# A four-layer megakernel: the first pair's split and first convolution made one stage earlier, and the second pair's moved among the edge products

## What is computed

```python
x = x + ffn0(cond0(x, cond_512))   # fp8-quantised 1024x1024 product
x = x + ffn1(cond1(x, cond_512))   # 1024x1024 product and a top-2 mixture of 16 low-rank experts
x = x + ffn2(cond2(x, cond_512))   # the same with sparsemax over 8 experts
x = x + ffn3(cond3(x, cond_512))   # low rank, gated (SiLU), low rank

def cond(x, style):                # TYPES = same, upsample, same, downsample
    for i, typ in enumerate(TYPES):
        x = layer(x, style, weights[i], biases[i], mod_w[i], mod_b[i], typ)
```

## Time and profile before

| | |
|---|---|
| median of 3 runs | 2204.11 us (2204.09 to 2206.6) |
| the profiled execution | 2207.09 us |
| its span in the trace | 2205.3 us |
| TensorE busy | 2032.4 us, 92% |
| VectorE, ScalarE, GpSimd busy | 54%, 40%, 18% |
| mean granted TensorE clock | 0.964 of full speed |

### The profile page before, as it was taken

One profiled execution on the slowest core, in us unless ns is written; L12 is line 12 of the kernel. 1 busy time (PEld: TensorE's weight loads), 2 busy tenths in 40 slices (PEclk: granted clock), 3 DMA queues, 4 the chain that ended last, 5 costly groups with the idle time before them and its releaser, 6 DMA issues. The chain is left out here.

```text
span 2205.3 us, 29894 instructions
## 1 busy us (share of the span) xinstructions
PE 2032.4 (92%) x9742; PEld 1665.3 (76%) x9750; DVE 1183.8 (54%) x1986; ACT 885.6 (40%) x1366; POOL 388.3 (18%) x463
## 2 busy tenths in 40 slices
PE   4899956899999979997999999988999999979998
PEld 4777723788888868886788888867888778858886
DVE  6888888745445443224644445436555444454443
ACT  4577722444433321002433333324666544413441
POOL 4122211111111100012111111111000033342334
PEclk9999989899999989997999999998999999989999
DMA  7666546321112232224311111212111011132114
GB/s 185 187 182 181 167 162 216 101 75 57 57 57 71 63 124 76 77 95 135 99 57 57 57 57 61 63 49 81 29 38 33 15 53 50 46 132 78 50 43 156
DMA packets 96302, 196.97 MB, mean 89 GB/s; under 512 B 16768, under 2 KB 46976, under 8 KB 95488
## 3 DMA queue, kind: packets, MB, share of 16 engines
q1 hardware_dynamic: 94976, 194.40, 28.2%
q10 hardware_dynamic: 1280, 1.97, 0.4%
HBM read 142.27 MB, written 54.07 MB: 89 GB/s over the span
## 5 line engine op out<-in xcount | busy, mean ns | idle before, releaser
L936 PE MATMUL ps<-l_u_hi,l_g_hi 128*128 128x512 f32 x512 | 208.9, 408 | 15.7 <-DVE l_u_lo L1270 10.1
L1100 ACT ACTIVATE l_hs<-ps,l_EY,dem3e 128x512 f32<-128x512 f32 x128 | 99.2, 778 | 302.4 <-PE ps L936 292.4
L936 PE MATMUL ps<-l_u_lo,l_g_hi 128*128 128x512 f32 x512 | 204.7, 400 | 0.0
L936 PE MATMUL ps<-l_u_hi,l_g_lo 128*128 128x512 f32 x512 | 204.2, 399 | 0.0
L119 POOL TENSOR_TENSOR l_hs<-l_EY,ones 128x4 f32<-128x4 f32 x128 | 35.0, 273 | 860.1 <-ACT l_hs L1100 860.1
L989 PE MATMUL ps<-l_w_hi,l_h_hi 128*128 128x512 f32 x512 | 167.7, 409 | 0.0
L989 PE MATMUL ps<-l_w_lo,l_h_hi 128*128 128x512 f32 x512 | 163.7, 401 | 0.0
L989 PE MATMUL ps<-l_w_hi,l_h_lo 128*128 128x512 f32 x512 | 163.1, 400 | 0.0
L2228 POOL TENSOR_TENSOR f_a_lo<-f_prod,f_a_hi 128x512 fp32r<-128x512 f32 (+1 forms) x88 | 113.8, 1293 | 269.2 <-ACT f_a_hi L2131 269.2
L2184 DVE SCALAR_TENSOR_TENSOR f_prod<-ps,b,f_gate 128x512 f32<-128x512 f32 (+1 forms) x88 | 66.0, 750 | 170.0 <-ACT f_gate L2124 170.0
L1270 DVE SCALAR_TENSOR_TENSOR l_u_lo<-ps,s_u,l_u_hi 128x512 fp32r<-128x512 f32 x128 | 95.5, 749 | 89.1 <-ACT l_u_hi L1082 88.9
(11 more groups left out here) (326 smaller groups left out, 4892.3 us busy)
## 6 DMA issues: line engine op xcount, KB each, us to landing
xin<-x SPq DMA_DIRECT2D x96, 256.0 KB, 4.0
l_xr<-x SPq DMA_DIRECT2D x32, 512.0 KB, 4.6
x<-l_xr SPq DMA_DIRECT2D x32, 512.0 KB, 2.6
v<-in_ffn_v SPq DMA_DIRECT2D x84, 128.0 KB, 2.7
xin<-in_x SPq DMA_DIRECT2D x16, 512.0 KB, 5.5
xb<-in_x SPq DMA_DIRECT2D x16, 512.0 KB, 3.2
x<-xb SPq DMA_DIRECT2D x16, 512.0 KB, 2.6
q_xr<-x SPq DMA_DIRECT2D x16, 512.0 KB, 3.9
```

What stands on the lines that cost most here:

```text
L936: mm = nc.tensor.matmul(ps[:, 3 + h, :], Gs[ws][:, h, at:at + P], Us[ms][:, h, 1 + q:1 + q + HALF], start=(k == 0), stop=(k == 11))
L1100: nc.scalar.activation(hs[:, h, :], ps[:, 3 + h, :], ACT.Identity, bias=EY[:, 1, 0, bass.ds(h * NP + p, 1)], scale=dem3e[:, bass.ds(h * NP ...
```

## The change

It has five parts.

1. `Xs`, `Zs` and a tile `rows` become constants of the whole program. At the end of `fp8_ffn`, `expert_delta` and of layer 2's conv phase, ScalarE (`split_first_hi`) and VectorE (`split_first_lo`) make the splits of x and z for pair 0 of the layer that follows, and TensorE (`first_conv0`) its first convolution. In layers 1 to 3 the phase itself then begins without them.
2. The waits for the last stores at the end of `fp8_ffn`, `expert_delta` and the conv phases go. In their place there are waits in the next stage: SP's ahead of the load of the bias, ahead of the pack (`c_raw`), GpSimd's ahead of a memset, ScalarE's ahead of hs, VectorE's ahead of `expert_delta`'s first output.
3. In every layer's first pair `weights_a(1)` and the first half of pair 1's convolution (`conv0_half(1, 0)`) come before `edges_p`, the second half behind `edges_v`, and `weights_a(2)` before `edges_y`. VectorE makes x_lo of pair 1's first half ahead of its part of `edges_u`; ScalarE waits for `m_done` before `read_u(1, h)`.
4. TensorE waits for the memsets (`zeros_ready`) before `weights_g(0)` in layers 1 to 3, and GpSimd no longer clears the borders of `Xs` there.
5. Several tiles share memory: `hs`, `xr`, `bias_n`, `ve_f` and the outputs of the feed-forward stages are parts of `rows`.

```diff
+    def split_first_lo(self, nc, dve, n, sem):
+
+        for h in range(2):
+            dve.wait_ge(sem("xh_ready"), 2 * NP * n + h + 1)
+            nc.vector.scalar_tensor_tensor(self.Xs[1][:, h, 1:HALF + 1], self.xin[:, h, :], self.s_x[:, n, h:h + 1],
+                                           self.Xs[0][:, h, 1:HALF + 1].bitcast(F32), ALU.mult,
+                                           ALU.subtract).then_inc(sem("xl_ready"), 1)
...
+    def first_conv0(self, nc, pe, ps, n, sem):
+
+        pe.wait_ge(sem("clo_ready"), n)
+        pe.wait_ge(sem("ul_ready"), 2 * NP * n)
+        for h in range(2):
+            pe.wait_ge(sem("xl_ready"), 2 * NP * n + h + 1)
+            k = 0
+            for t in range(2):
+                for ws, ms in PASSES:
+                    mm = nc.tensor.matmul(ps[:, h, :], self.c_part[ws][:, B0 + t * P:B0 + (t + 1) * P],
+                                          self.Xs[ms][:, h, t:t + HALF], start=(k == 0), stop=(k == 5))
+                    k += 1
+            mm.then_inc(sem("c0_done"), 1)
...
             if with_ffn:
+                sp.wait_ge(sem(("q_stored0", "e_stored0")[layer - 1]), 8 * NP)
                 sp.dma_start(bias_n[:, :], d[f"ffn{layer}_bias"].partition_broadcast(P)).then_inc(bias_loaded, 16)
...
             if with_ffn:
                 store(NP - 1)
-                sp.wait_ge(x_stored, 16 * (r0 + NP))
...
-            pe.wait_ge(zeros_ready, 2 * layer + 1)
-            if layer > 0:
-                pe.wait_ge(clo_ready, layer)
-            conv0(0)
+            if layer == 0:
+                pe.wait_ge(zeros_ready, 1)
+                conv0(0)
             weights_a(0)
             edges_u()
+            pe.wait_ge(zeros_ready, 2 * layer + 1)
             weights_g(0)
...
                 if first:
+                    weights_a(1)
+                    conv0_half(1, 0)
                     edges_p()
-                    weights_a(1)
                     main(0)
                     edges_v()
-                    conv0(1)
+                    conv0_half(1, 1)
+                    weights_a(2)
                     edges_y()
                     weights_g(1)
                     transpose_h(0)
-                    weights_a(2)
...
+                act.wait_ge(m_done, 2 * g0 + 1)
                 read_u(1, 0)
+                act.wait_ge(m_done, 2 * g0 + 2)
                 read_u(1, 1)
...
-            split_x(0)
+            if layer == 0:
+                split_x(0)
             edges_x()
-            split_z(0)
+            if layer == 0:
+                split_z(0)
             read_u(0, 0)
             read_u(0, 1)
             read_a(0)
             split_z(1)
+            split_x_half(1, 0)
             dve.wait_ge(zeros_ready, 2 * layer + 2)
             edges_u()
             some_maxima(1)
             sum_g(0)
-            split_x(1)
+            split_x_half(1, 1)
             split_g(0)
...
             quantise(NP - 1, 1, False)
             finish(NP - 2, 0, False)
+            K.split_first_lo(nc, dve, 1, sem)
             finish(NP - 1, 1, False)
```

More of the change, by code:

```diff
@@ L147, in __init__, with split_first_hi @@
         self.c_raw = tile("c_raw", [P, CW])
+        self.Xs = [tile("x_hi", [P, 2, HALF + 2], F32R), tile("x_lo", [P, 2, HALF + 2], F32R)]
+        self.Zs = [tile("z_hi", [P, 2, TAPS, C], F32R), tile("z_lo", [P, 2, TAPS, C], F32R)]
+        self.rows = tile("rows", [P, 2, L])
+    def split_first_hi(self, nc, act, n, sem):
+        act.wait_ge(sem("x_loaded"), 32 * NP * (n - 1) + 32)
+        act.wait_ge(sem("c0_done"), 2 * NP * n)
+        for h in range(2):
+            nc.scalar.activation(self.Xs[0][:, h, 1:HALF + 1], self.xin[:, h, :], ACT.Copy,
+                                 scale=self.s_x[:, n, h:h + 1]).then_inc(sem("xh_ready"), 1)
+        act.wait_ge(sem("a_done"), NP * n)
+        for h in range(2):
+            nc.scalar.activation(self.Zs[0][:, h, :, :], self.Z[:, n, :, :], ACT.Copy,
+                                 scale=self.s_v[:, n, h:h + 1]).then_inc(sem("zh_ready"), 1)
@@ L564, in conv_phase @@
         else:
-            stage = kept["b_raw"] if layer == 1 else sb("stage", [P, SLOTS, KB * SMALL[2] if layer == 2 else L])
+            stage = kept["b_raw"] if layer == 1 else sb("stage", [P, SLOTS if layer == 2 else 2, KB * SMALL[2] if layer == 2 else L])
         if with_ffn:
@@ L621, in conv_phase @@
         if with_ffn:
-            xr = sb("xr", [P, L])
+            xr = K.rows[:, 0, :]
         chunks = []
@@ L760, in _ @@
                     load_chunk(k)
+                if layer == 3:
+                    sp.wait_ge(sem("x_stored"), 16 * r0)
+                else:
+                    for s in range(2):
+                        sp.wait_ge(sem(("q_stored", "e_stored")[layer - 1] + str(s)), 8 * NP)
             if with_ffn:
@@ L1052, in _ @@
             over_pairs(pe, iteration)
+            if layer == 2:
+                K.first_conv0(nc, pe, ps, 3, sem)
             if layer == 3:
@@ L1176, in first_pair @@
                     act.wait_ge(sem("p_packed_away"), 48)
+                elif layer < 3:
+                    act.wait_ge(sem(("q_stored1", "e_stored1")[layer - 1]), 8 * NP)
                 read_h(0, 0)
@@ L1221, in iteration @@
                     next_weights()
+                    if layer == 2:
+                        K.split_first_hi(nc, act, 3, sem)
                 if layer > 0:
@@ L1457, in tail @@
                     v.tensor_copy(tau[:, 0:1], tau[:, 0:1]).then_inc(small_read, 1)
+                if layer == 2 and isinstance(p, int) and p == NP - 1:
+                    K.split_first_lo(nc, dve, 3, sem)
                 if with_ffn:
@@ L1573, in _ @@
             g = nc.gpsimd
-            for t in Xs:
-                step(g.memset(t[:, :, 0:HALF + 2:HALF + 1].bitcast(F32), 0.0))
+            if layer == 0:
+                for t in Xs:
+                    step(g.memset(t[:, :, 0:HALF + 2:HALF + 1].bitcast(F32), 0.0))
             step(g.memset(g_f[0:C, :, 0:C], 0.0))
@@ L1683, in _ @@
             store(NP - 1, 1)
-            for s in range(2):
-                sp.wait_ge(stored[s], 8 * NP)
         @block.gpsimd
@@ L1703, in _ @@
             turns(act, body)
+            K.split_first_hi(nc, act, 1, sem)
         @block.vector
@@ L1787, in expert_delta @@
         xr = sb("xr", [P, 2, L])
-        xo = sb("xo", [P, 2, L])
+        xo = K.rows
         b_dram = d["ffn1_b"].rearrange("(k p) o -> k p o", p=P)
@@ L1911, in finish @@
                 dve.wait_ge(xr_loaded[s], 8 * (p - s) + 16)
+                if first and s == 0:
+                    dve.wait_ge(sem("x_stored"), 16 * NP)
                 if not first:
@@ L1984, in gated_ffn @@
         prod = sb("prod", [P, 2, HALF])
-        asp = [sb("a_hi", [P, 2, HALF], F32R), sb("a_lo", [P, 2, HALF], F32R)]
+        asp = [t[:, :, 0:HALF] for t in K.Xs]
         zsp = [sb("z_hi", [P, 2, T], F32R), sb("z_lo", [P, 2, T], F32R)]
         xr = sb("xr", [P, NT, L])
-        xo = sb("xo", [P, 2, L])
+        xo = K.rows
         (const_loaded, w_hi, w_lo, v2_hi, v2_lo, gu_done, silu_ready, prod_ready, ah_ready, al_ready,
```

55 lines of the change are left out of this document (35 added, 20 removed).

## The result

The changed kernel takes 2198.13 us (median of 10 runs, 2195.07 to 2200.84), the kernel before 2204.27 in the runs made beside it (10 runs, 2199.76 to 2208.04). The ratio is 0.9971, 95% interval 0.9962 to 0.9980: 6 us faster. The number forecast was 2192.7 with a range of 2185 to 2200. So the sign and the range held, and the size was half of what the sum gave. The profiled execution took 2199.35 us (span 2197.5), 7.7 less than that of before.

A forecast was written before the change was run, and what follows sets the result against it. TensorE, busy 92% of the span, was taken as the bound, leaving its idle and low-clock stretches. Terms summed to -11.4 us, taking the profiled 2207.09 to 2195.7 us and the median to 2192.7; range 2185 to 2200.

The forecast's parts named there:

- layer 1 to its expert stage: Boundary into the expert stage: only the store wait goes, so the stage starts sooner, -2.4 us.
- layer 1, last product to main(0): Layer 1's start: no boundary gain, but main(0) at 394.4 against 396.60, -2.2 us, bounds -4 and 0.
- layer 2: Layer 2's start, boundary included: main(0) at 1040.4 against 1042.92, -2.5 us, bounds -4.5 and -1.
- layer 3: Layer 3's start, boundary included: pair 1's load goes out earlier, main(0) at 1503.15 against 1509.47, -6.3 us.
- layer 0 (to the fp8 stage's last product): Layer 0's first pair: new order delays the dense stretch 1.0 us, clock fall adds 1: +2.0 us, bounds 0 and +3.5.
- The boundaries: Phase starts: store waits go, first convolution precedes the 0.3 us barrier; layer 3 starts 1.1 us earlier, layer 1 gains nothing.
- Pair 1's load: First pairs, layers 1 to 3: x's load gates the work before main(0); layer 2's split 11.84 us behind the phase start.
- rival (c): Pair 1's load lands 3 us later in layers 1 to 3, cancelling the gain: 2201.7 us; chance 0.15, milder forms included.
- From the split to main(0): Layers 1 to 3, pair 1's x split to main(0): 10.4, 10.85 and 11.25 us, with VectorE blocked beside GpSimd's chunks.
- "The links are the same" behind main(0): Layers 1 to 3, main(0) to first ffn product: VectorE's chain starts earlier by as much, later links unchanged, so 0 us.
- "Each shift reaches the end whole": Rest of the program: loops are unchanged and bound by TensorE, so every shift carries whole into the total time.
- Rival (d): TensorE's new idle places in first pairs bring more half-clock stretches: five more give 2205 us, seven 2210; chance 0.06.

The follow-up runs named there:

- e9: Kernel before with the gated stage's tiles a_hi and a_lo two elements wider per half, unused: 1.0001 of before.
- e10: Kernel before with an unused tile of 16 bytes per partition ahead of all stage tiles: 0.9992 of before.
- e1: Changed kernel with layer 0's first pair back in the order of before: 2196.6 us, 0.9965 of before.
- e4: Changed kernel with ScalarE's half of the first weight chunk ahead of its split of pair 1's x in layers 1 to 3: 2194.6 us, 0.9959 of before.
- e7: Changed kernel with the first pair of layers 1 to 3 back in the order of before: 2196.4 us, 0.9964 of before.
- e3: Changed kernel with the waits for the last stores restored at the ends of the conv, fp8 and expert stages: 2203.0 us, 0.9995 of before.
- e2: Changed kernel with pair 1's x load issued first in layers 1 to 3, ahead of bias and chunks: 2188.3 us, 0.9930 of before.
- e11: Changed kernel plus layer 0's old order, pair 1's load in the preceding stage, chunks behind split_g(0) (2177.3 us); GpSimd's first chunks held until the edge chain ends: 2183.0 us.

## Why the prediction was right in sign and wrong in size

By its own terms, in the two profiled executions (the time saved was 6.1 us by the medians, 7.8 between these two):

| term | predicted | measured |
|---|---|---|
| layer 1 to its expert stage | -2.4 | -2.3 |
| layer 1, last product to main(0) | -2.2 | -0.1 |
| layer 2 | -2.5 | -1.5 |
| layer 3 | -6.3 | -4.8 |
| behind main(0), layers 1 to 3 | 0 | +3.9 |
| layer 0 (to the fp8 stage's last product) | +2.0 | +3.2 |
| sum | -11.4 | -1.6 |

**The boundaries: right.** Counted from the last product, the phases start as forecast: layer 3 3.06 us behind it (3.2 predicted), layer 1 4.8 behind the fp8 stage's (4.7), the expert stage's wait 5.64 to 3.36 us.

**Pair 1's load: the step that failed.** From the phase's start to the split of pair 1's x I put 9.5, 11.84 and 6.2 us; they were 12.75, 13.07 and 8.41, 6.7 us more in all. This is rival (c), at three quarters of its size. The kernel before already showed part of it. Its own load, from issue to landing of each of its two parts, in layers 1, 2 and 3:

```profile
DMA to landing us min/median/max: 6.0/6.4/6.7
...
DMA to landing us min/median/max: 7.7/8.1/8.4
...
DMA to landing us min/median/max: 4.5/4.8/5.1
```

The second part is issued 0.6 to 1.0 us behind the first and lands last, and the split waits for it. I counted 5.2 or 5.4 us, taken from another load, from the issue of the first part (in layer 1 with two more for the queue). Pair 0's load I had read in the same way: it was there at 369.9 and not at 369.4. From the phase's start to the landing of the second part it is, in us:

| kernels | layer 1 | layer 2 | layer 3 |
|---|---|---|---|
| put in the prediction | 9.5 | 11.8 | 6.2 |
| before, e9, e10 | 9.9 to 11.5 | 11.4 to 11.8 | 7.9 to 8.2 |
| changed, e1, e4, e7 | 12.1 to 13.5 | 10.5 to 13.0 | 8.1 to 8.4 |
| store waits back (e3) | 9.8 | 12.3 | 8.1 |

So three things differ. In layer 1 the distance grew, by 2 to 3 us. In e3, with the waits back, it is that of before, so the growth comes with the start that no longer waits for the store; whether the store's own traffic makes it, no run tells apart. I had named that store as what speaks for (c), and dismissed it as "one transfer beside five". In layer 2 the distance did not change beyond its scatter, and I took it rightly; the changed kernel's 13.0 is the longest of four. In layer 3 I counted on a load issued 1.3 us earlier that lands as much earlier. It was issued earlier, and landed no nearer to the phase's start than before. What holds it there no run tells apart; it stands behind two chunks in both kernels. e2 shows what the place behind the bias and the chunks is worth in all three: in layer 1 4.2 us instead of 8.8 from issue to landing, and the split 5.1 us behind the phase's start instead of 12.75.

**From the split to main(0): right.** 10.4, 10.85 and 11.25 us predicted, 9.1, 10.9 and 10.7 measured, collisions included; 1.8 us less in all.

**"The links are the same" behind main(0): wrong, by 3.9 us.** From main(0) to the first ffn product it was 22.54, 23.54 and 21.32 us, and became 24.62, 24.60 and 22.06. In layer 1 the loss is there in all four kernels with the new order and the load in its place (changed, e1, e3, e4: 24.0 to 24.7 us, against 22.5 to 23.6 in before, e9 and e10). In layer 2 it is not sure: e1, with the same code there, has 23.1, so up to 1.1 of the 3.9 us is scatter. In layer 1 1.7 us are seen on one row: GpSimd's third chunk, pushed behind main(0), meets the chain of the edge pass there (timeline of layer 1).

```profile
395.57 2.38 POOL L1669 TENSOR_TENSOR l_w_lo<-b_raw,l_w_hi 128x1024 fp32r<-128x1024 f32 x1 [1.01 <-ACT l_w_hi L1166]
...
396.42 2.07 DVE L1306 SCALAR_TENSOR_TENSOR x_lo<-xin,s_x,x_hi 128x512 fp32r<-128x512 f32 x1
...
398.63 3.24 POOL L1669 TENSOR_TENSOR l_w_lo<-b_raw,l_w_hi 128x1024 fp32r<-128x1024 f32 x1 [0.68 <-ACT l_w_hi L1166]
...
400.03 2.15 DVE L1395 TENSOR_TENSOR l_pe_f<-l_pe_f,be2e 64x288 f32<-64x288 f32 x1
...
402.70 0.45 DVE L1395 TENSOR_TENSOR l_pe_f<-l_pe_f,be2e 64x288 f32<-64x288 f32 x1
```

The 2.15 us stand against 0.45 for the same instruction at 402.70. The rest I have not traced row by row; `weights_a(2)` and `conv0_half(1, 1)` now stand in front of `edges_y` there.

The rows agree with the rule of the Trainium skill's page "SBUF — State Buffer" (section on the two sides) that the prediction drew on, which says: whichever of the two starts first holds the shared pair for its whole instruction. Its two conditions (two SBUF inputs, or a fast mode that uses two ports) fit as well. ue_hi, a cast with one input, was held up (2.42 us for 0.36 in layer 2); between 384 and 864 elements such a cast's time grows by 0.25 us (0.36 to 0.61), that of the two-input instructions on the same tiles by 0.50 (0.56 to 1.06), so it runs at twice the rate. And `sum_g`, one of whose inputs lies in PSUM, ran its 1.22 us beside a chunk.

**Layer 0: right at its place, 1.2 us small.** `edges_y` came 1.15 us later (1 predicted), and another 1.2 followed up to the transposes. e1 puts 2.4 us on the order at the fp8 stage's last product, in one execution of each; the other 0.8 is less than two executions differ by there (before and e10: 2.5).

**"Each shift reaches the end whole": right in the loops of layers 0 to 3 (0.3 us in all), wrong elsewhere.** What is missing between -1.6 and the -7.8 of the two spans is -6.2 us that the sum didn't know: -4.2 at the ends of layers 1 and 2, -1.9 in the expert stage, -1.5 in the gated stage, +1.0 between the first ffn product and the second pair's transposes, +0.3 in the loops, and 0.1 of rounding. The largest is chance in the kernel before: from pair 14's transposes to layer 1's last product its profiled execution took 44.4 us, and the 13 other kernels took 41.2 to 42.9, with no edit there that bears on it. TensorE's granted clock was 0.80 of full in before's last 17 us of that layer and 0.89 in the last 15.3 here, behind waits of the same 2.37 us. Before's profiled execution was 3.0 us above its median, as the prediction says without asking where.

So the range held partly by luck, on gains that I had not forecast. Rival (d) did not come: the mean granted clock is 0.965 against 0.964.

## What to carry to other kernels

When a change takes away the work in front of a load's first reader, the load does not come forward with it, and one that was just hidden becomes the gate. Read its landing from the trace of the kernel before, of its last part and in its own place, instead of carrying over the time of another load. Then give it a place by what waits for it; here one moved line was worth 9.8 us, more than the change, and nothing in the kernel before. And where one engine's instructions hold up another's, count them all: moving one into idle time helps only if the next does not take its place (e4, e11).
